# Where GpSimd sends its indirect transfers in a gated recurrence with routed experts

## What is computed

```python
def step(carry, xs):                      # 128 steps, over time
    r, state = carry
    qt, kt, vt = xs
    r = decay * r + kt * vt
    retained = (qt * r).reshape(B, D)
    inp = retained @ Wi.T + bi
    gate = jax.nn.sigmoid(inp @ Wg.T + bg)
    blended = gate * state + (1.0 - gate) * inp
    state = jnp.tanh(blended @ A.T + inp @ Bm.T)
    out = state @ Wo.T + bo
    return ((r, state), out)

shared_out = _swiglu(fx @ w_shared_in) @ w_shared_out
top_val, top_idx = jax.lax.top_k(softmax(fx @ w_gate + gate_bias), 2)
hid = _swiglu(fx @ w1_shared)
routed_out = sum over e of wdense[:, e] * (hid @ w2[e])

x = x + tanh(g_xattn[0]) * recurrence(layernorm(x), ctx, ctx, ...)
x = x + tanh(g_ffn[0]) * (shared_out + routed_out)(layernorm(x))
```

## Time and profile before

| | us |
|---|---|
| median of 3 runs | 520.9 (518.39 to 521.04) |
| the profiled execution | 519.97 |
| its span, first to last instruction | 518.2 |
| TensorE busy (matmul) | 434.6 (84%) |
| VectorE busy | 364.1 (70%) |
| ScalarE busy | 221.7 (43%) |
| GpSimd busy | 184.9 (36%) |
| scatters L1823, x48, and gathers L1836, x48: GpSimd busy | 49.8 and 49.6 |
| ScalarE idle before the 128 tanhs of L959 | 183.6 |

### The profile page before, as it was taken

How to read it: one execution, slowest core, us unless ns; L and a number is a source line. 1 busy time by engine, 2 the same in 40 slices (tenths; PEclk the granted TensorE clock), 3 DMA queues, 4 the chain that set the end, 5 groups by cost and what they waited for, 6 DMA issues and landing times.

```text
span 518.2 us, 12156 instructions
## 1 busy us (share of the span) xinstructions
PE 434.6 (84%) x4324; PEld 355.5 (69%) x4324; DVE 364.1 (70%) x1303; ACT 221.7 (43%) x520; POOL 184.9 (36%) x225
## 2 busy tenths in 40 slices
PE   5977799999997959999988898879869979968660
PEld 4965688878885748898877777778756747645320
DVE  3687887989797857777776775767837865406865
ACT  3655555667564625464545444536232313212100
POOL 3012302224136374111154554442454370520632
PEclk9998899999999998999999999999989989979986
DMA  7783234052251221874642349647331365832424
GB/s 162 209 222 111 41 104 119 15 144 45 101 135 52 63 82 38 168 123 113 132 115 96 99 97 180 143 129 128 123 103 52 81 154 134 200 113 73 139 80 148
DMA packets 102571, 59.14 MB, mean 114 GB/s; under 512 B 74352, under 2 KB 92784, under 8 KB 102512
## 3 DMA queue, kind: packets, MB, share of 16 engines
q1 hardware_dynamic: 97776, 45.77, 36.7%
q0 software_dynamic: 4736, 12.59, 7.9%
HBM read 23.74 MB, written 25.56 MB: 95 GB/s over the span
## 4 chain that ended last, share of the span: by engine, by line
PE 46%; DVE 24%; issue 10%; another core or an unknown queue 7%; ACT 5%; POOL 2%; DMA 1%; POOLq 0%; DVEq 0%; ACTq 0%
PE bank L576 12%; PE bank L565 10%; PE bank L623 5%; PE rec L709 5%; PE rec L590 4%; DVE u_hi L1268 4%; PE rec L623 3%; PE rec L595 2%; DVE u_full L1270 2%; DVE r L1371 2%; PE rec L565 1%; PE bank L842 1%; ACT state L959 1%; DVE ret L1384 1%
## 5 line engine op out<-in xcount | busy, mean ns | idle before, releaser
L959 ACT ACTIVATE state<-rec 128x64 f32<-128x64 f32 x128 | 36.6, 286 | 183.6 <-PE rec L595 138.5
L1268 DVE SCALAR_TENSOR_TENSOR u_hi<-gt,state 128x64 f16<-128x64 f32 x127 | 44.6, 351 | 86.7 <-ACT state L959 73.5
L590 PE MATMUL rec<-u_hi,a_hi 128*128 128x32 f16 x512 | 48.8, 196 | 28.4 <-DVE u_hi L1268 20.5
L1836 POOL DMA_INDIRECT yg<-yrows,slots_i x48 | 49.6, 1034 | 56.0 <-issue 35.5
L1823 POOL DMA_INDIRECT hrows<-hid_rows,slots_i x48 | 49.8, 1037 | 53.6 <-issue 25.3
L590 PEld LDWEIGHTS rec<-u_hi,a_hi 128*128 128x128 f16 x512 | 37.5, 99 | 38.0 <-DVE u_hi L1268 25.9
L590 PE MATMUL rec<-u_hi,a_lo 128*128 128x32 f16 x512 | 48.3, 195 | 1.0 <-issue 1.0
L1766 POOL TENSOR_TENSOR hs_lo<-hs,hs_hi 128x512 f16<-128x512 f32 x15 | 17.4, 1163 | 72.4 <-ACT hs_hi L1160 71.6
L590 PEld LDWEIGHTS rec<-u_hi,a_lo 128*128 128x128 f16 x512 | 35.9, 99 | 3.7 <-issue 1.8
L595 PE MATMUL rec<-u_lo,a_hi 128*128 128x32 f16 x512 | 36.8, 196 | 1.5 <-issue 0.5
L565 PE MATMUL bank<-xn_hi,sh_hi 128*128 128x256 f16 x128 | 34.9, 273 | 0.0
(11 more groups left out here) (291 smaller groups left out, 1419.6 us busy)
## 6 DMA issues: line engine op xcount, KB each, us to landing
yrows<-squares_sh SPq DMA_DIRECT2D x18, 256.0 KB
x_sb<-in_x_dram SPq DMA_DIRECT2D x16, 256.0 KB, 3.3
c_sb<-in_ctx_dram SPq DMA_DIRECT2D x64, 64.0 KB
xr_sb<-in_x_dram SPq DMA_DIRECT2D x16, 256.0 KB
hrows<-zeros SPq DMA_DIRECT2D x4, 1024.0 KB, 5.7
yrows<-squares_w SPq DMA_DIRECT2D x15, 256.0 KB
raw_w<-in_L_ffn_w_dram SPq DMA_DIRECT2D x8, 256.0 KB, 4.4
out_dram<-raw_w SPq DMA_DIRECT2D x8, 256.0 KB
```

Source lines behind the costliest of these rows:

```text
L590: pe.matmul(o[:, oc, :], w[:, kc, oc * P:(oc + 1) * P], u_hi[t % 2][:, kc, :], start=False, stop=False, skip_group_check=True)
L959: act.activation(step_of(state[i % 2], t), step_of(rec[i % 2], t), ACT.Tanh, scale=1.0 / PSCALE).then_inc(st_ready, 1)
L1268: dve.scalar_tensor_tensor(out=u_hi[p][:, :, :], in0=gate, scalar=1.0, in1=old, op0=ALU.add, op1=ALU.mult).then_inc(uh_ready, 1)
L1836: pool.indirect_dma_start(yg[t % 4][:, s, pick, :], None, yrows[q % 2], bass.IndirectOffsetOnAxis(ap=slots_i[q][:, at:at + 1], axis=0), bo ...
```

## The change

GpSimd's transfers get eight places in an iteration, one behind each recurrence step. In iterations up to 15 each of them waits for the tanh of its own step. Scatters of a group fill two whole iterations with one transfer for each step, gathers of group 1 likewise; the gathers of groups 2 and 3 stand two to a place in iterations 16 and 17, where no tanh is waited for. `hs_lo` now stands behind the transfers of steps 0 and 1, the first layer norm's root behind that of step 2, the second's and the hidden rows' low half behind that of step 3, and the transfers of steps 4 to 7 at the end. The first duo of group 3 moves from (15, 5) to iteration 16, whose six slots now hold two each, and the waits that its old place needed go.

```diff
-              + [(14, slot) for slot in (0, 1, 2)] + [(15, 5)] + [(16, slot) for slot in range(5) for _ in range(2)] + [(16, 5)])
+              + [(14, slot) for slot in (0, 1, 2)] + [(16, slot) for slot in range(6) for _ in range(2)])
...
-                return bank[3 if slot == 5 and first.dense(i - 2) else {0: 5, 1: 3, 2: 5, 3: 4, 5: 5}[slot]][:, :]
+                return bank[{0: 5, 1: 3, 2: 5, 3: 4, 5: 5}[slot]][:, :]
...
-                    elif first.dense(i - 2):
-                        pe.wait_ge(lg_ready, i - 1)
...
-                        pe.wait_ge(y_ready, evacuated(15, 5))
...
-            spread(SCATTERS, range(0, 4), [(5, 1)] * 2 + [(6, 0)] * 3 + [(6, 1)] * 4 + [(7, 0)] * 4 + [(7, 1)] * 3)
-            spread(SCATTERS, range(4, 8), [(9, 1)] * 2 + [(10, 0)] * 3 + [(10, 1)] * 4 + [(11, 0)] * 4 + [(11, 1)] * 3)
-            spread(GATHERS, range(0, 4), [(12, 0)] * 4 + [(12, 1)] * 5 + [(13, 0)] * 5 + [(13, 1)] * 2)
-            spread(SCATTERS, range(8, 12), [(13, 1)] * 3 + [(14, 0)] * 4 + [(14, 1)] * 5 + [(15, 0)] * 4)
-            spread(GATHERS, range(4, 8), [(15, 1)] * 4 + [(16, 0)] * 4 + [(16, 1)] * 8)
-            spread(GATHERS, range(8, 12), [(17, 1)] * 16)
+            def slots(*iterations, each=1):
+                return [(i, t) for i in iterations for t in range(STEPS) for _ in range(each)]
+            spread(SCATTERS, range(0, 4), slots(6, 7))
+            spread(SCATTERS, range(4, 8), slots(10, 11))
+            spread(GATHERS, range(0, 4), slots(12, 13))
+            spread(SCATTERS, range(8, 12), slots(14, 15))
+            spread(GATHERS, range(4, 8), slots(16, each=2))
+            spread(GATHERS, range(8, 12), slots(17, each=2))
...
-                if spot == 0 and i < TILES and ((i, 0) in SCATTERS or (i, 0) in GATHERS):
-                    pool.wait_ge(st_ready, STEPS * i + 1)
+                if i < TILES and ((i, t) in SCATTERS or (i, t) in GATHERS):
+                    pool.wait_ge(st_ready, STEPS * i + t + 1)
...
                 moves(i, 0)
+                moves(i, 1)
...
+                moves(i, 2)
                 x_rstd(f, k)
+                moves(i, 3)
...
+                moves(i, 4)
...
-                moves(i, 1)
+                for t in range(5, STEPS):
+                    moves(i, t)
```

More of the change, by code:

```diff
@@ L1846, in spread, with moves @@
                     plan.setdefault(at, []).append(row)
-            spread(SCATTERS, range(0, 4), [(5, 1)] * 2 + [(6, 0)] * 3 + [(6, 1)] * 4 + [(7, 0)] * 4 + [(7, 1)] * 3)
-            spread(SCATTERS, range(4, 8), [(9, 1)] * 2 + [(10, 0)] * 3 + [(10, 1)] * 4 + [(11, 0)] * 4 + [(11, 1)] * 3)
-            spread(GATHERS, range(0, 4), [(12, 0)] * 4 + [(12, 1)] * 5 + [(13, 0)] * 5 + [(13, 1)] * 2)
-            spread(SCATTERS, range(8, 12), [(13, 1)] * 3 + [(14, 0)] * 4 + [(14, 1)] * 5 + [(15, 0)] * 4)
-            spread(GATHERS, range(4, 8), [(15, 1)] * 4 + [(16, 0)] * 4 + [(16, 1)] * 8)
-            spread(GATHERS, range(8, 12), [(17, 1)] * 16)
-            def moves(i, spot):
-                if spot == 0 and i < TILES and ((i, 0) in SCATTERS or (i, 0) in GATHERS):
-                    pool.wait_ge(st_ready, STEPS * i + 1)
[L1859 to L1862, removed]
+            def slots(*iterations, each=1):
[6 more added lines that the diff above has]
+            spread(GATHERS, range(8, 12), slots(17, each=2))
+            def moves(i, t):
+                if i < TILES and ((i, t) in SCATTERS or (i, t) in GATHERS):
+                    pool.wait_ge(st_ready, STEPS * i + t + 1)
+                for row in SCATTERS.get((i, t), ()):
+                    scatter(*row)
+                for row in GATHERS.get((i, t), ()):
+                    gather(*row)
             def iteration(i, k):
```

## The result

| | before | changed |
|---|---|---|
| median of 20 runs, us | 521.06 | 523.09 |
| profiled execution, span, us | 518.2 | 521.3 |

The ratio is 1.0055, 95% interval 1.0029 to 1.0081: the changed kernel is slower by about half a per cent. I had forecast 519.0 us, a hair faster. The time lies inside the range of 506 to 538, but on the other side of the kernel before.

What follows compares the result with a forecast made beforehand. The recurrence, then a TensorE tail, was taken to bound the kernel, with rows of GpSimd transfers delaying TensorE's completions. -30 + 8.2 + 8.3 + 3.4 - 1.3 + 9.5 = -1.9 gave 519.0 us, range 506 to 538.

Steps and rivals of the forecast that it cites:

- rows removed, spread transfers added: Iterations 6, 7, 10 to 15: ending rows of 72 transfers saves 30 us; one transfer in each of 64 steps costs 8.2.
- late first duos of iterations 8 and 12, with the clock: Last scatters wait for the last tanh, so duos start 4.5 and 3.8 us late: 8.3, plus 3.4 for the clock.
- duo out of iteration 15: Group 3's duo leaves iteration 15's recurrence, -1.3 us, and lengthens the tail by 1.3.
- tail: Behind the recurrence: later first duo 4.9, clock 1.7, moved duo 1.3, more gathers 1.6; 9.5 us longer.
- the duo can start 7.5 us after the last tanh: Chain from last tanh through scatter and transposes to a group's first duo, in iterations 8, 12 and the tail: 7.5 us.
- The clock's part: Idle TensorE before late duos loses its clock: 3.4 us at 1.2 instead of 2.4 GHz, costing 1.7 us each.
- GpSimd's own work is not held up: Low halves and rstd steps need results 2 us or more behind the tanh, and a transfer takes 1.0: no cost.
- The price that I said decides: Spread transfers in 64 steps: the change breaks even at 0.16 us each; forecast 0.13.
- rival of the full iterations: Where TensorE is busy 98%, 40 transfers in iterations 10 and 12 to 15 cost 0.46 each: 530.6 us, chance 0.12.
- Slower: Total chance 0.41: 0.06 within the forecast's range, full iterations 0.12, fixed price 0.17, another cause 0.06.
- free transfers: Rival: a transfer alone costs nothing, only rows cause lateness: 510.8 us, or 505.7 without clock losses; chance 0.27.
- The last rival: Transfers do not cause the late tanhs, which stay; only late starts are added: 540.8 us, chance 0.06.

Runs made afterwards that it cites:

- experiment 1: The changed kernel with the scatters of groups 1 and 2 ending two steps earlier, behind step 5 of iterations 7 and 11: 509.99 us, ratio to before 0.974.
- experiment 2: The kernel before with one wait added, holding the last scatter of groups 1 and 2 until the last tanh of iterations 7 and 11: 538.88 us, ratio 1.028.
- experiment 8: Experiment 7's second kernel with all transfers of step 3 moved behind the layer-norm roots and the hidden rows' low half: 500.57 us, ratio 0.958.
- experiments 4 and 5: Experiment 1 with scatters of groups 1 and 2 and gathers of group 1 sent in pairs (519.86 us, ratio 0.993) or in fours (532.70 us, 1.018).
- Experiment 7: First, the changed kernel with group 3 as before: 524.97 us. Second, experiment 1 with group 3's scatters also two steps earlier: 503.57 us, ratio 0.963.
- experiment 3: The changed kernel with the last scatter of groups 1 and 2 behind step 6, beside the one before it: 513.45 us, ratio 0.983.

## Why the prediction was wrong

By its own steps, in the profiled execution (measured lengths of iterations; for what iteration 12 would take without a late start, experiment 1's 25.2):

| step | forecast | measured |
|---|---|---|
| rows removed, spread transfers added | -30 + 8.2 = -21.8 | -22.9 |
| late first duos of iterations 8 and 12, with the clock | 8.3 + 3.4 = 11.7 | 9.0 + 8.2 = 17.2 |
| duo out of iteration 15 | -1.3 | not measured, taken as is |
| tail | 9.5 | 9.6 |
| ahead of iteration 6 | 0 | 0.5 |
| sum | -1.9 | +3.1 |

**The step that failed is "the duo can start 7.5 us after the last tanh".** It takes 9.64 and 9.28, and 9.26 in the tail. Three of its four parts were read from rows in which something else had already run:

- The start of the scatter. I took 0.30 behind the tanh's end from the earlier trace rows; it is 0.79. In that row GpSimd was busy with another transfer until 183.70, so 0.30 was the gap between two transfers, not the time from a semaphore to a waiting engine.
- The scatter to the transposes. 2.43 became 3.54, because the transfer itself took 2.08 instead of 0.98. It starts as VectorE's decay scan does (206.10, 1.35 us), and ends 0.78 us behind it. The four scatters of the changed kernel that start 0.05 to 0.24 us behind a scan's start, at 157.57, 206.15, 287.81 and 308.88, took 2.04 to 2.09. A gather at 341.48, 0.02 behind a scan's start, took 1.00, and its scan 1.41; why it is spared is open. No run moves the scan, so the cause is argued from these coincidences. A sign of it stood in the earlier trace rows, where a transfer 0.7 us behind a scan's start took 1.53. In the tail, where no scan stands, it took 0.97, and the transposes came 2.42 behind it. The Trainium skill, page "SBUF — State Buffer", section "🔬 SBUF: two separate sides", describes something like it: GpSimd makes the descriptors of its own DMAs, and can't write them while VectorE runs an operation in one of its two-port modes, which holds the SBUF ports that both share. The trace agrees in that the scatters end only behind the scan, 1.1 us later than alone; that the scan is such an operation no run shows.
- The transposes to the duo. 4.47 became 5.02, 4.66 and 5.76.

With the slack of 1.05 and 1.8 us the duos are 6.6 and 5.6 us late. The clock's part was under-sized too: 5.3 us of work at 0.50 behind the idle 6.5, where I had 3.4 from a stretch behind 2.26 us of idle time. That is 2.6 instead of 1.7 us each. Queued behind the duo, and without slack to win it back, was right: experiment 1 takes 16.5 us off the two iterations, and experiment 2's held scatters add 9.1 and 6.6 to them and 14.6 to the time.

**The first line came out right in part by luck.** Spread transfers cost 0.03 us each where I forecast 0.17, and with a price so low the removed rows gave some 25, not 30. I had looked for 22 to 23 us in iterations 6 and 7; they took 26.8 and 24.1. Iteration 7 still has a row: `w_lo` holds GpSimd until 184.0, so the transfers of steps 5 to 7 of iteration 6 and 0 and 1 of iteration 7 follow each other and the tanh at 191.36 is 2.5 us late (6.9 forecast, 4.3 gained). And iteration 6, from which I took 3.0, got 1.1 us longer. I had written that GpSimd's own work is not held up; the root behind step 3's transfer is (experiment 8). Of the rest, iterations 10 and 14 gave more (3.5 and 5.9) than read from peers (1.5 and 5.3).

**The price that I said decides, 0.16 us for a spread transfer, decides nothing.** At a price of zero my sum gave 510.8; the kernel took 523. What decided was a term that I gave no range at all, the 7.5 us: each microsecond on it counts at three places. (A slip beside it: by the sum's own numbers the rival of the full iterations breaks even with the kernel before at 0.22 us per transfer, not 0.24.) So the rivals were all drawn around the wrong unknown. "Slower" got 0.41, but through mechanisms that the runs refute; free transfers together with a longer chain were not among the rivals.

**The last rival**, that transfers are not the cause of the late tanhs, is refuted: spread out, the transfers leave one tanh of iterations 6 to 15 over 2 us late where the kernel before has several, and in experiments 4 and 5 rows bring the late tanhs back. The sentence of the Trainium skill, page "SBUF — State Buffer", section "Who interferes with whom", that a DMA never contends with a compute engine does not cover what is seen here: beside rows of GpSimd's transfers, TensorE's completions come late.

**The tail** was forecast at 9.5 and measured at 9.6, but the match is partly luck. Its first duo came 9.3 us behind the last tanh, not 7.5, which is 6.6 us later than before and not 4.9, so the other terms (the clock, the twelfth duo, the gathers) were too large by 1.6 together. Experiment 7 took 6.7 us off the tail by moving the scatters alone.

## What to carry to other kernels

A queue of small transfers beside a full engine should be spread, one at a time, and that is nearly free; but the last one of a batch has a consumer, and its deadline is the consumer's start less the whole chain: wake-up, descriptors, landing, the load behind it. Work the schedule back from there before spreading forward. A duration read where the engine was already running is not the one that a waiting engine will show, and a chain that stands in the sum three times deserves a range of its own. Look as well at what small operation stands behind each inserted transfer in its engine's queue, here one transfer of 1.03 us ahead of a root, which cost 0.8 us in an iteration where the clock held, and a pair, which cost 4.3 where it fell.

## What the runs showed of the hardware

- Rows of indirect transfers from GpSimd make TensorE's completions late, and the lateness grows with the row: in iteration 13, with eight transfers each time, 27.1 us for single ones, 28.1 for pairs and 30.5 for fours, the latest tanh 0.4, 1.4 and 2.7 us behind its matmuls. A single one can do it too (0.88 us, beside the gather of 326.04), but most don't. Which resource they share stays open. A version with half the bytes in each transfer, which would tell bytes from descriptors, was not tried.
- A scatter that starts 0.05 to 0.24 us behind the start of VectorE's scan of 1.35 us takes 2.04 to 2.09 us, alone 0.97; a gather 0.02 behind one took 1.00.
- After a stop of 6.5 us TensorE's next work ran at 1.2 GHz instead of 2.4, for 5.3 us in iterations 8 and 12 and for 3.8 us in the tail. After 2.94 us of idle time in experiment 3 the first 1.1 us of work still ran at 2.4, the 3.4 us behind it at 1.2.
